# Attentions 0 and 2 of a four-layer kernel: TensorE's row-score units move between the keys or values and the score tiles that reuse their banks

## The reference, cut to what matters

```python
q = (x @ Wq).reshape(B, N, HEADS, hd).transpose(0, 2, 1, 3)
k = (context @ Wk).reshape(B, M, HEADS, hd).transpose(0, 2, 1, 3)
v = (context @ Wv).reshape(B, M, HEADS, hd).transpose(0, 2, 1, 3)
scores = jnp.einsum('bhid,bhjd->bhij', q, k) * scale
attn = jax.nn.softmax(scores, axis=-1)
out = jnp.einsum('bhij,bhjd->bhid', attn, v)
out = out.transpose(0, 2, 1, 3).reshape(B, N, DIM)
return out @ Wo
```

## Time and profile before

| | |
|---|---|
| median of 3 runs | 5375.91 us (5374.27 to 5377.44) |
| the profiled execution | 5381.54 us, span 5379.8 us |
| busy | PE 4389.9 us (82%), DVE 3489.0 us (65%), ACT 2280.1 us (42%), POOL 982.4 us (18%) |
| attention 0, its steady part | 300 to 1150 us of the span |
| attention 2, its steady part | 3930 to 4780 us of the span |
| the span's queues | DMA queue q1: 294.71 MB |

### The profile page before, as it was taken

The page is one execution under the profiler, slowest core; times in us unless marked ns, Lnnn a source line. Parts: engine busy times, 40 slices in busy tenths (PEclk is TensorE's granted clock), DMA queues, the critical chain, the costliest instruction groups (busy, mean ns, idle before and its releaser), DMA issues. The chain is left out here.

```text
span 5379.8 us, 99448 instructions
## 1 busy us (share of the span) xinstructions
PE 4389.9 (82%) x34185; PEld 3734.3 (69%) x34185; DVE 3489.0 (65%) x6058; ACT 2280.1 (42%) x4584; POOL 982.4 (18%) x750
## 2 busy tenths in 40 slices
PE   4299999985689998999899938777599999987694
PEld 4177777764588888888888836555477777765573
DVE  4477777765665566566656637776677777765545
ACT  0056666652233333333333315554356666653341
POOL 0011111112110111010101006554311111112320
PEclk7599999997799999999899968877799999998897
DMA  7244444420111001000100020000144444420292
GB/s 240 64 102 103 107 103 95 101 57 9 44 25 23 17 21 26 21 21 17 26 21 21 4 63 0 0 0 1 25 102 101 108 107 96 100 57 24 49 184 51
DMA packets 190536, 314.81 MB, mean 59 GB/s; under 512 B 132372, under 2 KB 140870, under 8 KB 190406
## 3 DMA queue, kind: packets, MB, share of 16 engines
q1 hardware_dynamic: 186822, 294.71, 24.1%
q10 hardware_dynamic: 3584, 18.43, 0.9%
HBM read 146.07 MB, written 19.54 MB: 31 GB/s over the span
## 5 line engine op out<-in xcount | busy, mean ns | idle before, releaser
L1221 PE MATMUL a1m_ps_o<-a1m_cn,a1m_prob_t 125*128 125x97 f32 x5376 | 654.7, 280 | 0.2 <-issue 0.2
L1221 PEld LDWEIGHTS a1m_ps_o<-a1m_cn,a1m_prob_t 125*128 125x128 f32 x5376 | 642.6, 198 | 0.4 <-issue 0.4
L1362 ACT ACTIVATE a1m_prob<-a1m_ps_s,a1m_neg_max 128x500 f32<-128x500 f32 x672 | 405.8, 675 | 558.2 <-DVE a1m_neg_max L1300 558.2
L1297 DVE TENSOR_REDUCE a1m_bank_max<-a1m_ps_s 128x1 f32<-128x500 f32 x672 | 455.6, 679 | 146.6 <-PE a1m_ps_s L1187 145.3
L1187 PE MATMUL a1m_ps_s<-a1m_cxt,a1m_qhi 98*128 98x500 f32 x1344 | 436.7, 406 | 6.7 <-DVE a1m_qlo L1289 5.0
L809 ACT ACTIVATE a2m_prob_t<-a2m_ring 125x448 f32<-125x448 f32 x768 | 384.2, 546 | 122.9 <-PE a2m_ring L494 121.4
L809 ACT ACTIVATE a0m_prob_t<-a0m_ring 125x448 f32<-125x448 f32 x768 | 384.1, 546 | 122.3 <-PE a0m_ring L494 120.8
L705 DVE TENSOR_REDUCE a2m_bank_max<-a2m_ps_s 112x1 f32<-112x1000 f32 x256 | 303.0, 1184 | 143.0 <-PE a2m_ps_s L543 142.4
L705 DVE TENSOR_REDUCE a0m_bank_max<-a0m_ps_s 112x1 f32<-112x1000 f32 x256 | 303.0, 1184 | 140.3 <-PE a0m_ps_s L543 139.6
L1203 PE MATMUL a1m_ps_t<-g_ident,a1m_prob 128*125 128x128 f32 x2688 | 375.0, 276 | 0.4 <-ACT a1m_prob_t L1370 0.3
L1370 ACT ACTIVATE a1m_prob_t<-a1m_ps_t 125x512 f32<-125x512 f32 x224 | 133.8, 597 | 551.5 <-PE a1m_ps_t L1203 551.4
(11 more groups left out here) (786 smaller groups left out, 9483.2 us busy)
## 6 DMA issues: line engine op xcount, KB each, us to landing
a0m_ks<-a0m_k_hi SPq DMA_DIRECT2D x256, 187.5 KB
a2m_ks<-a2m_k_hi SPq DMA_DIRECT2D x256, 187.5 KB
a0m_ks<-a0m_k_lo SPq DMA_DIRECT2D x128, 187.5 KB
a2m_ks<-a2m_k_lo SPq DMA_DIRECT2D x128, 187.5 KB
ctx_t<-cprep_tr ACTq DMA_DIRECT2D x32, 562.5 KB
a0m_raw<-ctx_t SPq DMA_DIRECT2D x32, 562.5 KB
a1m_raw<-ctx_t SPq DMA_DIRECT2D x32, 562.5 KB
a2m_raw<-ctx_t SPq DMA_DIRECT2D x32, 562.5 KB
```

What stands on the lines that cost most here:

```text
L1221: m = pe.matmul(ps_o[at, 0:CO], prob_t[:, u % 2, t, at], cn[:, h, t, :], start=(t == 0), stop=(t == KT - 1))
L1297: dve.tensor_reduce(bank_max[:, s, k:k + 1], ps_s[:, k, 0:BK], AX.X, ALU.max).then_inc(bank_maxed, 1)
L1362: act.activation(prob[:, s, k * BK:(k + 1) * BK], ps_s[:, k, 0:BK], ACT.Exp, bias=neg_max[:, s:s + 1]).then_inc(exped, 1)
```

## The change

Only the order within `half` changes, on two engines; every instruction, tile and semaphore stays. On TensorE X0 goes ahead of `unit(0)`; T3 goes behind `denominators` and `unit(1)`; `unit(2)` and T6 go ahead of `round_of(0)`; and in the queries half `queries` goes behind X1. On VectorE the low part of the first third goes ahead of the first maxima, and the query instructions behind the low part of the second third.

```diff
@@ TensorE, half(i, h)
                 turned_of(0, 1)
                 if among(m - 1, halves):
                     sums(m - 1, (h - 1) % 4 // 2, (h - 1) % 2, 2)
+                extra(0)
                 unit(0)
-                extra(0)
                 turned_of(2)
+                extra(1)
                 if h == 1 and among(i + 1, NP):
                     queries(i)
-                extra(1)
-                turned_of(3)
                 if among(m - 1, halves):
                     denominators(i, h)
                 unit(1)
+                turned_of(3)
                 extra(2)
                 turned_of(4, 5)
+                unit(2)
+                turned_of(6)
                 round_of(0)
-                turned_of(6)
-                unit(2)
                 turned_of(7)
```

## The result

The changed kernel takes 5502.22 us (median of 4 runs, 5497.62 to 5510.33) against 5375.09 for the kernel before: a ratio of 1.0236, 95% interval 1.0224 to 1.0248, or +127 us where +56 was forecast. The profiled execution took 5500.33 us, its span 5498.6 against 5379.8. The direction was forecast, the size lies outside the range.

The account below looks back on a forecast made before the run. TensorE was taken as nearly full, its T6 waits set by an unbroken VectorE row. Per attention 15 x (1.13 + 0.20) + 31 x 0.26 = 28 us, 56 in both, gave 5432 us, range 5398 to 5460.

Parts of the forecast that it names:

- It's the start that costs: Queries half: VectorE's unbroken row starts at 1.67 with a low part instead of 0.74 with a maximum, T6 0.93 later.
- Left is the exchange of round and unit, +0.20: Plain keys half: T3's wait only moves ahead of the third unit; exchanging round and unit makes the half 0.20 longer.
- +0.26: Values halves: the third unit waits for the second one's maximum, T7 comes at 8.07 against 7.81, 0.26 later.
- T6 in the queries half at 9.83: Queries half: T6 starts 9.83 us after the half's start, against 8.90 before, at the end of VectorE's row.
- the three terms: Lengthening per half: queries 1.13, plain keys 0.20, values 0.26; 28 us per attention, 56 in both.
- The bounds for these prices: Exchange 0.13 or 0.20, values halves' third unit losing 0.05 to 0.6; total 28 to 92 us, lower part held likelier.
- Rival C: The new 1.7 us wait in queries halves lowers TensorE's clock, T6 some 3.6 us later: +108 more, 5540; chance 0.03.
- The rest at nothing: ScalarE's slack, SyncE's spreading of keys and the earlier overwrite of k_hi add no time anywhere else.
- T6 again 8.02: Plain keys half: the reciprocal starts at 4.55 as before, so T6 stays 8.02 us into the half.
- T6 still waits for L698 in both keys halves: Sign of being right: T6 keeps its wait for the low part (L698) in queries and plain keys halves.
- Rival B: Gains and losses cancel: plain keys halves lose all their wait, values halves cost 0.13 instead of 0.26; 5382; chance 0.08.
- Rival A: The cover works: waits for L698 vanish and nothing takes their place, -66, 5310; chance 0.07.

Follow-up runs that it names:

- e5: Kernel before with only X0 put ahead of the first unit, on TensorE and VectorE: 5396.38 us, 1.0036.
- b1: Kernel before with denominators ahead of T3; on VectorE in keys halves, reciprocal behind the last low part, output sums behind the third unit's maxima: 5319.95 us, 0.9897.
- e4: Kernel before with only T3 put behind denominators and the second unit on TensorE: 5369.37 us, 0.9986.
- e3: Kernel before with only the third unit and T6 put ahead of the round on TensorE: 5483.55 us, 1.0198.
- e2: Changed kernel with queries ahead of X1 again on TensorE, and ahead of the second low part on VectorE: 5464.92 us, 1.0168.
- e1: Changed kernel with VectorE's order of before, TensorE's order staying changed: 5473.01 us, 1.0170.
- e6: Kernel before with the changed order in keys halves only, on both engines; values halves as before: 5465.73 us, 1.0172.
- e7: Changed kernel with T3 ahead of denominators in queries halves only: 5477.41 us, 1.0188.
- b2: b1 with queries also late: behind the second round on TensorE, between the third unit's maxima and output sums on VectorE: 5381.13 us, 1.0017.
- b4: b2 with VectorE's output sums ahead of its query instructions: 5314.70 us, 0.9889.

## Why the prediction was right in kind and wrong in size

- **"It's the start that costs": shown.** e5 has this alone and measures +1.01 in a queries half for +0.93. The row, the place of the new wait and its length (1.76 for "about 1.7") stand in the trace as forecast. That the row on VectorE, and no neighbour of T6, is what TensorE waited for is shown from the other side by b1: with the row one instruction shorter the waits vanish and 56 us come back, close to the 66 that the earlier trace rows put on them (14 of the 56 may be T3's place, by e4).
- **"Left is the exchange of round and unit, +0.20", and the values halves' "+0.26": the steps that failed.** The exchange of round and unit was mis-sized twofold. By e3 it costs 0.4 in each keys half, and in the changed kernel's values halves +0.52. The distances were taken from neighbours of another kind. From T6 to the round it is 0.41 (487.62 to 488.03), not 0.30; from T7 to the shifts behind it 0.31 (488.93 to 489.24), where T7 behind a unit had 0.22. Each handover is 0.1 longer, and there are two: 0.40. In a values half the third unit starts 6.12 after X0 (forecast 6.05), T6 is 0.90 behind it (forecast 0.82), T7 1.21 later, and the same 0.31 follows.
- **T6 in the queries half at 9.83: it came at 10.12.** L508 takes 1.10 when it starts the half and not 1.00, so the low part starts 0.09 late; the reciprocal starts 6.52 instead of 6.36; and from the second maximum to the low part it is 0.69 (486.20 to 486.89), not 0.58, since the third there was late. In sum 0.29.
- At the full clock the three terms were 1.13 + 0.20, and 0.26, and measured 1.64 + 0.48, and 0.52 (in the marks 1.63, 0.49, and 0.52 to 0.64). With the prediction's own counts 15 x 2.12 + 31 x 0.52 = 48 in each attention, 96 in both, not 56. That is 40 of the 71 us that are missing. The bounds for these prices were right in kind (the upper one was 92), and I chose the lower part of them because of a single row.
- **Rival C, "the clock falls", at 0.03: wrongly set aside.** It came in 12 of the 112 halves counted and costs 21 us, not 108. The argument against it was that 1.7 is nearer to 1.2 and total idle hardly changes. The idle did change: TensorE has 63 us of it in the 850 us of attention 0, and had 47. And e3 falls behind waits of 0.9 and less, the changed kernel mostly doesn't behind 1.76, and the kernel before never does behind 1.17. A rival with a partial outcome should have had a partial price; it was priced as all or nothing.
- **"The rest at nothing": wrong by a gain at the start of an attention**, 6.2 us in attention 0 and 0.9 in attention 2 here, 9 and 7 in e5. X0 ahead of the first unit takes a third out of the queue behind a DMA; the larger share goes with the granted clock there, as e2 shows against the changed kernel.
- **"T6 again 8.02" in the plain keys half: right by luck.** It is 8.10, but the sign "T6 still waits for L698 in both keys halves" failed there: T6 doesn't wait, the third unit ahead of it does.
- **Rival B, loss cancelled in the plain keys half: refuted**, they are 0.48 longer. But e4 shows that its ground was real: with `denominators` ahead of T3 alone the half gets 0.47 shorter. The prediction saw this idle time of 0.38 and let it go, because it comes back as the third unit's wait; that holds for the changed order and not for the old one.
- **Rival A: refuted**, but the waits for L698 did all but vanish (2.8 us of 31.8). "Nothing takes their place" is what failed, as forecast.

The Trainium skill, "TensorE: Matmul & The Clock Gate", section "A second HAM failure mode: psum-queue depth-cycling", says of a kernel in bf16 that small idles among groups that cycle through PSUM banks can make the clock swing. The changed kernel, e1, e3, e6, e7 and b2 agree, with 2 to 9 halves in an attention; before, e4, e5, b1 and b4 cycle through the same banks and stay at 1.00 in their steady parts, and e2 does but for one fall in its last pair.

## What to carry to other kernels

When an engine waits for another one, find the whole unbroken row of instructions that ends with the release; moving the waiting work away only moves the wait, and an instruction taken out of the row wins it back. An exchange of two steps on a full engine is priced by the handovers of the new neighbours; where the trace has no such pair, take the upper bound, and multiply by how often it comes before calling it small. Look at the first and last passes of a loop separately, and at the granted clock there before giving a gain to the order: what costs in the middle can win there.

## What the hardware showed unexpectedly

- The length of a wait alone doesn't tell whether the granted clock falls. It fell behind waits of 0.78 (changed, plain keys half), 0.91 (e3), 1.34 (b2) and 1.77 us (changed), each time to 0.50 for some 3 to 7 us, and didn't with 1.17 in every queries half (before) and 1.3 (e5). In the changed kernel 1.76 led to a fall in only some of the halves.
- What stands further back counts. The plain keys halves of e2 and of the changed kernel have the same order and the same wait of 0.78; in the changed kernel, with 1.76 instead of 1.2 in the queries halves between them, 6 of 28 fall, and in e2 none before the last pair. Which part of the work in between decides stays open.
- A fall costs less than its stretch: TensorE's instructions take 0.7 to 0.8 us more each, but T6 was 1.13 us late, since TensorE has slack behind VectorE's row there.
- The start-to-start distance of the same pair of matmul groups depends on what stands before them: the shifts start 0.22 or 0.31 behind T7.
